# A recurrence, its output rows and a gated network woven together: the rank of every block's side work

## The reference

```python
def L0_attn(x):                        # a recurrence over 1024 positions
    u = einsum('bsd,hd->bsh', x, W_in) + b_in           # hidden size 1024
    def step(state, u_t):
        s = tanh(u_t + state * gamma + beta)
        return s, s
    states = scan(step, 0, u over s)
    return einsum('bsh,dh->bsd', states, W_out) + b_out

def L0_ffn(x):                         # weights rounded to float8_e4m3fn
    gate = silu(x @ q(gate_w) * gate_scale)             # 512 -> 1536
    up = x @ q(up_w) * up_scale
    return (gate * up) @ q(down_w) * down_scale         # 1536 -> 512

x = x + layernorm(L0_attn(layernorm(x)))                # x1
x = x + layernorm(L0_ffn(layernorm(x)))
```

## Time and profile before

| | before |
|---|---|
| median of 3 runs | 558.2 us (555.98 to 560.86) |
| profiled execution | 558.66 us |
| its span | 556.8 us |
| mean granted TensorE clock | 0.993 |
| TensorE busy | 539.2 us, 97% |
| TensorE's weight loads busy | 457.0 us, 82% |
| VectorE busy | 446.4 us, 80% |
| ScalarE busy | 375.3 us, 67% |
| GpSimd busy | 228.7 us, 41% |

### The profile page before, as it was taken

How to read it: one execution, slowest core, us unless ns; L and a number is a source line. 1 busy time by engine, 2 the same in 40 slices (tenths; PEclk the granted TensorE clock), 3 DMA queues, 4 the chain that set the end, 5 groups by cost and what they waited for, 6 DMA issues and landing times.

```text
span 556.8 us, 11947 instructions
## 1 busy us (share of the span) xinstructions
PE 539.2 (97%) x2958; PEld 457.0 (82%) x2958; DVE 446.4 (80%) x2608; ACT 375.3 (67%) x2317; POOL 228.7 (41%) x372
## 2 busy tenths in 40 slices
PE   8998989989899999999999999999999999999995
PEld 5856769878689888889788988898888887899994
DVE  3699999978798998878897978878987888874414
ACT  3687687864578777877677768777676767762332
POOL 1221446474546533562319313642352322643532
PEclk9999989999999999999999999999999999999998
DMA  8789398972014200120003000210002000200011
GB/s 268 260 257 250 88 232 156 252 132 63 20 40 153 58 2 1 39 97 1 2 1 114 21 1 2 77 39 2 1 2 77 1 2 1 77 2 1 1 39 38
DMA packets 25333, 39.92 MB, mean 72 GB/s; under 512 B 3760, under 2 KB 8496, under 8 KB 25264
## 3 DMA queue, kind: packets, MB, share of 16 engines
q1 hardware_dynamic: 19904, 30.24, 16.6%
q0 software_dynamic: 4608, 8.39, 8.9%
q10 hardware_dynamic: 752, 0.54, 0.3%
HBM read 26.57 MB, written 4.20 MB: 55 GB/s over the span
## 4 chain that ended last, share of the span: by engine, by line
PE 69%; DVE 3%; ACT 1%; issue 0%; POOLq 0%; DVEq 0%; POOL 0%
PE gate_up L1131 26%; PE wide L1087 16%; PE wide L1161 13%; PE wide L1056 12%; PE wide L1107 1%; DVE recur L1231 1%; DVE recur_second L1231 1%; DVE fused L1364 0%; ACT pairs L1556 0%; ACT gated L1591 0%; DVE z L1377 0%; DVE stats_z L1245 0%; DVE x_lo L1346 0%; DVE x_res L1304 0%; DVE y L1281 0%
## 5 line engine op out<-in xcount | busy, mean ns | idle before, releaser
L1556 ACT ACTIVATE pairs<-recur 128x8 f32<-128x8 f32 x768 | 137.8, 179 | 90.1 <-DVE recur L1231 90.0
L1231 DVE TENSOR_TENSOR_SCAN recur<-recur,pairs 128x16 f32<-128x16 f32 x768 | 151.1, 197 | 48.1 <-ACT pairs L1556 45.6
L1556 ACT ACTIVATE pairs<-recur_second 128x8 f32<-128x8 f32 x768 | 137.3, 179 | 0.0
L1231 DVE TENSOR_TENSOR_SCAN recur_second<-recur_second,pairs 128x16 f32<-128x16 f32 x768 | 133.4, 174 | 0.0
L1754 POOL TENSOR_TENSOR fused_lo<-fused,fused_hi 128x256 fp32r<-128x256 f32 x95 | 70.8, 747 | 140.0 <-ACT fused_hi L1609 137.8
L1087 PE MATMUL wide<-w_out_sb,pairs 128*128 128x512 f32 (+1 forms) x272 | 113.0, 563 | 0.2 <-ACT pairs L1565 0.2
L1056 PE MATMUL wide<-x_norm_t,w_in_sb 128*128 128x256 f32 x448 | 101.9, 382 | 3.6 <-ACT x_norm_t L1507 3.6
L1056 PEld LDWEIGHTS wide<-x_norm_t,w_in_sb 128*128 128x128 f32 x448 | 84.8, 191 | 16.1 <-ACT x_norm_t L1507 4.3
L1087 PEld LDWEIGHTS wide<-w_out_sb,pairs 128*128 128x128 f32 x272 | 75.4, 298 | 25.0 <-ACT pairs L1565 0.7
L1161 PE MATMUL wide<-down_q,fused_hi 128*128 128x512 f32 x192 | 80.3, 418 | 1.6 <-POOL fused_lo L1754 1.6
L1591 ACT ACTIVATE gated<-gate_up,gate_scale_cols 128x128 f32<-128x128 f32 (+1 forms) x169 | 63.6, 379 | 26.7 <-PE gate_up L1131 26.4
(11 more groups left out here) (135 smaller groups left out, 777.9 us busy)
## 6 DMA issues: line engine op xcount, KB each, us to landing
x_res<-x SPq DMA_DIRECT2D x16, 256.0 KB, 3.3
x_in<-x SPq DMA_DIRECT2D x14, 256.0 KB, 4.6
out<-z SPq DMA_DIRECT2D x14, 256.0 KB, 2.5
x_norm_t<-x_t SPq DMA_DIRECT2D x5, 512.0 KB, 4.4
raw_own<-rounders POOLq DMA_DIRECT2D x9, 256.0 KB, 5.2
w_in_sb<-w_in_t SPq DMA_DIRECT2D x4, 512.0 KB, 7.0
w_out_sb<-w_out_t SPq DMA_DIRECT2D x8, 256.0 KB, 5.2
raw_own<-down_w SPq DMA_DIRECT2D x8, 256.0 KB, 4.7
```

Source lines behind the costliest of these rows:

```text
L1231: eng.tensor_tensor_scan(preact_of[b].rearrange("p c k -> p (c k)"), factors_of[b].rearrange("p c k -> p (c k)"), pairs[:, t % RING, colum ...
L1556: ins = eng.activation(pairs[:, t % RING + 1, columns, 0], preact_of[b][:, :, 1], ACT.Tanh)
```

## The change

Five tables of due steps get new numbers. The numbers that `timetable` gave as k on the side engines become tables of their own: `ROWS_RANK` for each tile's y and x1, `X1_RANK` for the copies of x1 turned, `CHUNKS_RANK` for gated, fused, fused_hi and fused_lo of a block, `Z_RANK` and `Z_COPY_RANK` for the down product's row work, `INPUTS_RANK` for u's copies. No operation is added or removed; lines behind the tables move down by 6. Three of the new tables are shown below and two of the old ones; a line of "..." stands for the others.

```diff
--- before.py
+++ after.py
@@ -147,11 +147,17 @@
 
 
 
-CHUNKS_FROM = [36.9, 268.9, 388.4, 510.8, 673.4, 840.2, 1054.2, 1034.2]
...
-INPUTS_FROM = [-1344.6, 58.5, 202.4, 260.9, 828.6, 579.7, 684.4, 999.7]
...
+CHUNKS_FROM = [72.0, -165.8, -368.4, 581.0, 427.8, 995.7, 723.3, 408.0]
...
+INPUTS_FROM = [-1067.2, -83.0, 307.1, 742.6, 572.3, 682.2, 882.0, 1348.8]
...
+ROWS_RANK = [220.1, -213.5, 83.9, -144.1, -286.0, -286.6, -582.2, -118.0, 162.5, 329.6, 4.1, 192.4, -17.4, 170.2, 475.1, -168.4]
...
+CHUNKS_RANK = [-359.3, -420.3, 464.7, -152.5, -422.8, -107.6, 383.0, -857.0]
...
+INPUTS_RANK = [-467.3, -96.3, -184.5, -275.4, -198.1, -16.2, -108.7, -188.0]
 TENSOR_MARGIN = 1.0
 GATE_UP_PIECES = 24
 TENSOR_FIRST = 16
@@ -474,10 +480,10 @@
             for b in range(batch):
                 transpose_x(n, b, -1.5)
         for m in range(KH // 2):
-            project_u(n, m, rank(n - 1, 4) if n > 1 else 3)
+            project_u(n, m, rank(n - 1, INPUTS_RANK[n]) if n > 1 else 3)
     for n in range(NB):
         for b in range(batch):
-            project_y(n, b, 60 if (n, b) == (0, 0) else -5 if n == 0 else rank(n, 6 + 2 * b))
+            project_y(n, b, 60 if (n, b) == (0, 0) else -5 if n == 0 else rank(n, ROWS_RANK[batch * n + b]))
     for p in range(NB):
         for b in range(batch):
             if p == 0:
@@ -488,7 +494,7 @@
                 scaled = [(v, 0.1) for v in rows("y", "y_copy", p, b)]
             if p > 0:
                 scaled += [(("gate_up", p - 1, KI - 1), 0.0)]
-            transpose_x1(p, b, scaled, rank(p, 4) if p > 0 else FIRST_X1_RANK)
+            transpose_x1(p, b, scaled, rank(p, X1_RANK[p]) if p > 0 else FIRST_X1_RANK)
         for i in range(KI):
             after = [(v, 0.2 - GATE_UP_STEPS / 2) for b in range(batch) for v in rows("low", "x1_low", p, b)] if i == 0 else []
             if i == 0:
@@ -497,12 +503,12 @@
                 after += converted(range(2 * i, 2 * i + 8))
             if p == 0 and i == 2:
                 after += converted(i for i in range(NP) if not by_transfer(i))
-            gate_up(p, i, after, (rank(p + 1, 4.5) if p > 0 else FIRST_CHUNKS_RANK) + 0.01 * i)
+            gate_up(p, i, after, (rank(p + 1, CHUNKS_RANK[p]) if p > 0 else FIRST_CHUNKS_RANK) + 0.01 * i)
             down(p, i, rank(p + 1, 7) + 0.1 * i, after=converted([GATE_UP_PIECES + i]) if p == 0 else ())
         for b in range(batch):
             if p < LAST:
-                norm_z(p, b, ("down", p, KI - 1), rank(p + 1, 20) if p > 0 else rank(2, 30),
-                       rank(p + 1, 4) if p > 0 else None)
+                norm_z(p, b, ("down", p, KI - 1), rank(p + 1, Z_RANK[p]) if p > 0 else rank(2, Z_RANK[0]),
+                       rank(p + 1, Z_COPY_RANK[p]) if p > 0 else None)
             else:
                 norm_z(LAST, b, (("down", "down_second")[b], LAST, KI - 1), rank(NB, 10 + b))
         if p + 2 <= LAST:
```

More of the change, by code:

```diff
@@ L146 @@
 DOWN_RANK, NEGATE_RANK, ISSUE_RANK, PEAK_RANK, FIRST_X1_RANK, FIRST_CHUNKS_RANK = 20.0, 0.0, -2.0, 150.0, -4.0, -3.0
-CHUNKS_FROM = [36.9, 268.9, 388.4, 510.8, 673.4, 840.2, 1054.2, 1034.2]
-CHUNKS_PER_BLOCK = [9.5, 13.5, 7.5, 5.5, 9.5, 7.5, 2.5, 7.5]
-INPUTS_FROM = [-1344.6, 58.5, 202.4, 260.9, 828.6, 579.7, 684.4, 999.7]
-ROWS_FROM = [63.7, 150.2, 105.8, 112.0, 335.2, 313.5, 548.2, 566.0, 566.8, 537.6, 813.5, 752.1, 805.6, 836.1, 1124.2, 933.4]
-ROWS_TURNED = [177.8, 96.6, 277.1, 157.6, 351.1, 503.1, 395.2, 481.6, 757.2, 721.7, 947.8, 826.2, 1022.5, 863.0, 1070.9, 1030.1]
+CHUNKS_FROM = [72.0, -165.8, -368.4, 581.0, 427.8, 995.7, 723.3, 408.0]
+CHUNKS_PER_BLOCK = [2.5, 53.5, 3.5, 7.0, 5.0, 13.5, 47.0, 34.5]
+INPUTS_FROM = [-1067.2, -83.0, 307.1, 742.6, 572.3, 682.2, 882.0, 1348.8]
+ROWS_FROM = [96.6, -167.0, -231.0, -104.0, 149.0, 403.9, -37.1, -137.6, 184.8, 314.3, 885.1, 367.5, 1035.2, 886.6, 1337.7, 1040.3]
+ROWS_TURNED = [-411.8, 194.1, 369.0, 301.1, -213.8, 297.8, 749.6, 720.3, 606.2, 703.6, 1203.0, 1363.4, 1086.5, 170.2, 651.3, 1257.2]
+ROWS_RANK = [220.1, -213.5, 83.9, -144.1, -286.0, -286.6, -582.2, -118.0, 162.5, 329.6, 4.1, 192.4, -17.4, 170.2, 475.1, -168.4]
+X1_RANK = [-340.6, -89.2, -378.6, -128.4, -0.5, 37.0, 159.5, 55.3]
+CHUNKS_RANK = [-359.3, -420.3, 464.7, -152.5, -422.8, -107.6, 383.0, -857.0]
+Z_RANK = [51.1, 174.3, -8.3, -27.2, -379.4, 81.9, 77.2]
+Z_COPY_RANK = [873.4, -342.5, 370.2, -274.7, -614.8, -49.4, 271.1]
+INPUTS_RANK = [-467.3, -96.3, -184.5, -275.4, -198.1, -16.2, -108.7, -188.0]
 TENSOR_MARGIN = 1.0
```

## The result

| | before | changed |
|---|---|---|
| median | 556.94 us (555.29 to 560.86, 22 runs) | 558.44 us (557.32 to 560.27, 22 runs) |
| profiled execution | 558.66 us | 559.72 us |
| its span | 556.8 us | 557.9 us |
| ratio to before | | 1.003, 95% interval 1.0016 to 1.0044 |

The change is slower by 0.3%, 1.5 us; forecast was 1.5 us faster. The two profiled executions alone do not show what happened, since that of before was a long one, 1.7 us over its median. The ratio goes by all runs.

The account below looks back on a forecast made before the run. Bound: TensorE's own work from 145 us; before that, only what both TensorE and the recurrence gain. 558.66 − 2.4 (early recurrence) + 0.9 (later steps) = 557.2, less 0.46 to the median: 556.7 us; range 553.0 to 561.3.

Parts of the forecast that it names:

- The third part: Steps 256 to 1024: VectorE and ScalarE placed ahead of products make the recurrence wait, most of it absorbed; +0.9 us.
- The fourth part: Behind the last step: both orders hold 51.9 us of TensorE's work and the same last products and sums; 0.
- Together 2.9 us: VectorE up to step 256: stalls at a late-weight conversion (1.70 and 0.36) and at a y copy (0.8) go.
- The base of the sum: Start of the forecast: profiled execution of 558.66 us, corrected by 0.46 to the 558.2 median of three runs.
- moved ones cost nothing as long as they don't wait: VectorE up to step 256: no conversion is added and one operation fits into a step, so moved conversions cost 0.
- The second rival: Early gain eaten by a late load or GpSimd's x_norm_t shifts near conversions of steps 206 and 218; 558.8 us, chance 0.22.
- A rule against the trace: Skill's rule that two SBUF inputs contend with GpSimd, which would slow x1's sum at step 236; no row showed it.
- −2.4: VectorE up to step 256: gain taken for the early recurrence in us, after 0.5 us kept back for close places.
- the one that no two scans stand over 1 us apart: Sign of being right: before step 256's scan, no two scans stand over 1 us apart.
- the sign for right and that for wrong: Start of step 256's scan: between 142.5 and 143.5 us if right, later than 145 us if wrong.
- TensorE before 145 us: TensorE up to the product needing step 255: 8.3 us go, clock's 1.0 included, 5.4 of new waits come; net −2.9.
- The forecast of new waits, 5.4: TensorE before 145 us: 1.0 for a rounding bank, 0.9 step 128, 1.3 y copy, 0.6 fused, 1.6 last fused_lo.

Follow-up runs that it names:

- shift early: Changed kernel with one GpSimd instruction, the shift of block 3's second half of x_norm_t, moved about 12 steps earlier; 555.89 us, ratio to before 0.9976.
- one input: Changed kernel with the second half of x1's sum at step 235 replaced by a statistic that reads one SBUF tile; 555.87 us.
- before, again: The kernel before, unchanged, run and profiled a second time; median 556.84 us.
- changed, again: The changed kernel, unchanged, run and profiled a second time; median 558.02 us.
- room: Kernel before with the last two conversions and what follows from them 6 steps later (the guard 30); 558.14 us, ratio 1.0008.
- due new: Changed kernel's five tables of due steps, with all ranks on VectorE, ScalarE and GpSimd as in the kernel before; 563.10 us.

## Why the prediction was wrong

**What held.** TensorE's work from the product that needs step 255 to the end is one length in every kernel with the tables of before or of the change behind it, 404.4 to 404.8 us, unless the clock fell. All that the change does is in when that product begins. The third part is so 0 at the end, not +0.9: between steps 256 and 1023 the recurrence loses 0.4 us (351.33 against 350.90 in the two second profiles), TensorE nothing. VectorE's wait for y there grew, but from 0.58 to 0.67 and not to 0.95, and its step, 658, took 1.16 us where that of before took 1.07:

```profile
331.09 0.29 DVE L1287 TENSOR_TENSOR y<-wide,b_out_rows 128x128 f32<-128x128 f32 x1 [0.67 <-PE wide L1093]
```

The fourth part held.

**The step that failed: "Together 2.9 us", VectorE's stream up to step 256.** It failed twice.

*Most of the gain was not of the order, but of one execution.* The stall at step 191 (1.70 + 0.36) and the wait for y (0.8) were in the profile of before, and with them its 256 steps took 128.84 us. The second profile of the same kernel has neither, and takes 125.77; the new order without its meeting takes 125.86. Neither profile of before is a typical one: 558.66 and 555.08 lie on both sides of the median. What the order gives over the median is what shift early shows on one chip, 555.89 against 556.87: 1.0 us (1.3 by the ratio), and not 2.4. Part of that 1.0 is the clock: 17 of the 29 runs of before there have a mean clock of 0.995 or less, with a median of 557.25, the other 12 have 556.09, and shift early has no such run. There was a sign of it: the three runs shown spread from 555.98 to 560.86. A stall for a transfer is the part of a profile that another execution need not repeat. The base of the sum was also 1.3 us too high, as the median of the three runs (558.2) turned into 556.94 with 22.

*The cost was among the rivals, and stood at nothing in the sum* ("moved ones cost nothing as long as they don't wait"). The second rival named the mechanism, GpSimd's shifts between steps 206 and 240 beside VectorE, and gave 558.8; measured is 558.44. It expected them at the conversions of steps 206 and 218; they met x1's sum at step 235. The price was 2.3 us of the recurrence, in place of 2.06, and 2.5 us of the time; that 558.8 lies so near is in part luck, as it holds the +0.9 that did not come. The prediction had put this meeting aside in "A rule against the trace", since no sum in the earlier trace rows took over 0.49. That row shows no sum that began while GpSimd was in a fused_lo or a shift; those that touched one began ahead of it (137.09, the fused_lo at 137.27). It was the absence of the case, and no evidence against the rule. The Trainium skill (GPSIMD Engine Reference, section Specifications) says that the two contend where VectorE has two SBUF inputs; one input, shift early and the 24 records of `fused` agree. The Trainium skill (SBUF — State Buffer, section Who interferes with whom) says that the loser blocks fully and isn't slowed: by that rule, the three sums that end 0.28 to 0.30 us behind GpSimd's end agree. The same section of the Trainium skill also says that whoever is first keeps the ports; here the sum's record starts at 132.38, the shift's at 132.93, and the sum was the one held. GpSimd was at a transfer's issue until 133.21, so its record may not show when it took hold of the ports; this stays open, and the measured 2.71 us decide.

*The clock was a follower.* The 2.3 us took TensorE's wait for fused_lo, just before its longest product, from 1.2 to 1.8 us, and in 2 of 5 executions the clock fell there: 1.4 us between the profiles, 1.8 to 2.5 between the groups, that no term had.

*The sum again, with the medians measured:* 556.94, less 1.0 for the early order, plus 2.5 for the meeting with the clock that follows it, plus 0 for the third part, is 558.4. Without the meeting the forecast of 1.5 us less would have looked nearly right, and by luck: of its two terms, −2.4 came as −1.0 and +0.9 as 0. Of its signs, the one that no two scans stand over 1 us apart failed (2.77 us at step 235), and step 256 at 144.88 stands between the sign for right and that for wrong.

**TensorE before 145 us.** It was to gain 2.9 net, 1.9 of it in waits and 1.0 in the clock. The waits lost 0.2 (7.7 against 7.5 us, from 20 us to the product); the clock's 1.0 did not come from the order alone, since before, again has no drop either. The forecast of new waits, 5.4, came as 7.7: 0.6 and 1.8 for the rounding banks where 1.0 was set, 2.1 for fused where 0.6 was, 0.9 for the copy of y where 1.3 was, 1.8 for fused_lo where 1.6 was and 0.5 for step 128 where 0.9 was. Of these, 1.8 hang on the meeting: with the shift early the sum of the waits is 5.95. In the new early order the product does not wait for step 255 itself. The wait that ends last is the one for fused_lo, and that follows the recurrence all the same, as the `fused` that it reads stands behind scan 249 in VectorE's stream: from scan 0, both `fused` and step 256 come 2.4 us earlier with the shift early than in changed, again.

**What stays open.** Why transfers are late in some executions: the old order's profiles have such waits at steps 191, 221 and, in room, 47 and 226, and moving two conversions did not help. With the shift early the 12 times spread over 1.4 us, where the 22 of before spread over 5.6. Part of that is the clock's drop at 78 us, which no profile of the new early order has; that the new order leaves its transfers more room would explain the rest, and was not tried apart. Nor is it shown what decides whether the clock falls after the same wait.

## What to carry to other kernels

A stall for a transfer in one profile is a sample: before its removal is counted as a gain, look whether the median and a second profile have it. When an order moves work of GpSimd, list what VectorE does with two SBUF inputs, or with a form like x1's norm (due new: 1.31 us in place of 0.39 beside a fused_lo), within a microsecond on either side, and move one of the two; here one instruction was worth 2.5 us. On a path of 0.48 us steps, a planner that keeps such operations apart by its own clock does not keep them apart on the chip: here it placed them 1.7 steps apart, and they met.

## What the runs showed of the hardware

- A sum of 256 columns with two SBUF inputs beside a GpSimd operation that reads SBUF took 0.73, 1.91 and 2.71 us in place of 0.46, each time to 0.3 us past the other's end; sums of 128 columns ended 0.15 us past it. Beside GpSimd's issue of a transfer alone the sum took 0.46, a statistic with one input took 0.40 beside both, and the same operation with one operand in PSUM took 0.49 at most, 24 times begun beside one.
- One SBUF input does not keep every form clear: x1's norm took 0.96 us in place of 0.39 at 511.6 us of the changed kernel, beside a fused_lo whose record begins 0.06 us after its own.
- The same wait of 1.8 us on TensorE was followed by the 1.2 GHz level in one profile of the changed kernel and by full clock in the other; the output product behind it took 8.46 or 7.07 us.
